# Recurrence with filler matmuls set one behind each group, and key and query work moved ahead of routing

## The reference

```
q, k, v = silu(causal_conv4(x @ Wq)), ... Wk, ... Wv;  beta = sigmoid(x @ Wb)      # x is layer-normed
q, k = l2norm per head;  per chunk: M = I + tril(beta k k^T, -1);  u, w = M^-1 (beta v), M^-1 (beta k)
per chunk in sequence:  u -= w S;  o = q S + tril(q k^T) u;  S += k^T u
y = rmsnorm(o) @ Wo;  x2 = x + layernorm(y);  h = layernorm(x2)
router: sigmoid scores, 3 of 8 groups, 4 of 32 experts, weights;  shared = (silu(h Wg) * (h Wu)) Wd
experts: gather by slot, silu(G) * U, down, weighted scatter-add;  out = x2 + layernorm(experts + shared)
```

## Time and profile before

| what | value |
| --- | --- |
| median of 3 executions | 1083.34 us |
| profiled execution | 1090.8 us |
| its span on the core | 1089.0 us |
| TensorE busy | 853.8 us (78%) |
| VectorE busy | 666.0 us (61%) |
| ScalarE busy | 367.1 us (34%) |
| mean granted TensorE clock | 0.892 of full |
| step part / expert part | to about 820 us / the rest |

### The profile page before, as it was taken

How to read it: one execution, slowest core, us unless ns; L and a number is a source line. 1 busy time by engine, 2 the same in 40 slices (tenths; PEclk the granted TensorE clock), 3 DMA queues, 4 the chain that set the end, 5 groups by cost and what they waited for, 6 DMA issues and landing times. The chain is left out here.

```text
span 1089.0 us, 31228 instructions
## 1 busy us (share of the span) xinstructions
PE 853.8 (78%) x13520; PEld 646.2 (59%) x13520; DVE 666.0 (61%) x1267; ACT 367.1 (34%) x683; POOL 117.5 (11%) x182
## 2 busy tenths in 40 slices
PE   6586697897889889889897988278693799999910
PEld 5465576665657676666665757146372688888800
DVE  2697498778569777977977976864238122212226
ACT  2523324533432543353453344112311112221215
POOL 1000000000000000000000000000001344454344
PEclk9886697999899989999999999779985899999965
DMA  8110002005100200200200020020006599999768
GB/s 272 62 42 2 4 1 81 4 1 201 61 5 1 100 4 2 79 23 3 69 33 2 1 81 4 1 78 4 26 33 251 190 362 361 360 346 360 253 153 241
DMA packets 48625, 113.15 MB, mean 104 GB/s; under 512 B 8576, under 2 KB 8704, under 8 KB 48368
## 3 DMA queue, kind: packets, MB, share of 16 engines
q1 hardware_dynamic: 42224, 96.50, 24.4%
q0 software_dynamic: 6272, 14.68, 6.2%
HBM read 84.34 MB, written 26.84 MB: 102 GB/s over the span
## 5 line engine op out<-in xcount | busy, mean ns | idle before, releaser
L463 PE MATMUL bank<-xnT,wring 128*128 128x256 f32 x768 | 168.9, 382 | 0.0
L463 PEld LDWEIGHTS bank<-xnT,wring 128*128 128x128 f32 x768 | 146.1, 191 | 23.7 <-issue 3.4
L1584 PEld LDWEIGHTS ps_g<-xgT,wring 128*128 128x128 f32 x1024 | 121.1, 194 | 17.2 <-issue 17.2
L1584 PE MATMUL ps_g<-xgT,wring 128*128 128x128 f32 x1024 | 121.5, 278 | 1.3 <-ACT xgT L1614 0.7
L992 DVE SCALAR_TENSOR_TENSOR cv<-pre,taps,cv 128x1024 f32<-128x1024 f32 x72 | 92.3, 1282 | 21.5 <-ACTq L757 20.3
L1717 DVE TENSOR_TENSOR hid<-ps_g,sg 128x160 f32<-128x160 f32 x32 | 10.4, 325 | 148.1 <-ACT sg L1624 104.1
L1493 POOL MEMSET xgT<- 128x512 f32 x2 | 1.0, 532 | 810.4 <-POOLq L1795 810.4
L555 PE MATMUL bank<-wo,o_ch 128*128 128x512 f32 x128 | 65.1, 667 | 20.6 <-DVE o_ch L1140 20.6
L596 PE MATMUL bank<-hT,su_w 128*128 128x256 f32 x256 | 72.8, 426 | 1.5 <-issue 1.5
L596 PE MATMUL bank<-hT,sg_w 128*128 128x256 f32 x256 | 68.3, 399 | 0.7 <-issue 0.4
L1614 ACT ACTIVATE xgT<-ps_x 128x320 f32<-128x320 f32 x32 | 14.0, 437 | 161.2 <-PE ps_x L1573 161.2
(11 more groups left out here) (189 smaller groups left out, 1420.6 us busy)
## 6 DMA issues: line engine op xcount, KB each, us to landing
wring<-in_ffn_W_gate SPq DMA_DIRECT2D x32, 512.0 KB
wring<-in_ffn_W_up SPq DMA_DIRECT2D x32, 512.0 KB
wring<-in_ffn_W_down SPq DMA_DIRECT2D x32, 512.0 KB
x_in<-in_attn_x SPq DMA_DIRECT2D x8, 512.0 KB, 3.8
x_res<-in_attn_x SPq DMA_DIRECT2D x8, 512.0 KB, 4.4
x_rows<-x SPq DMA_DIRECT2D x8, 512.0 KB, 2.8
h_rows<-h SPq DMA_DIRECT2D x8, 512.0 KB, 3.8
side_rows<-acc_sb SPq DMA_DIRECT2D x8, 512.0 KB, 5.2
```

The lines of the kernel that those rows point to most:

```text
L463: m = te.matmul(bank[:, c * COLS:(c + 1) * COLS], wqkv[:, w, kt, ct * P:(ct + 1) * P], xnT[:, kt, :], start=(kt == 0), stop=(kt == KT - 1))
L1584: m = te.matmul(ps_g[q % 2][:, (2 * a + i) * P:(2 * a + i + 1) * P], w[:, k, i * P:(i + 1) * P], xgT[q % 2][:, k, :], start=(k == 0), stop ...
```

## The change

It permutes the instruction lists of three engines and the order in which PSUM banks are handed out. No instruction is added or removed; only the places differ. `silu_kq`, `residual` and the like keep their code.

```diff
-ORDER = dict(begin="XPGX", one="PXOGW", two="PHEXFIOGW", loop="PHVYEXFIOGW", seven="PHVYEFIOGW", end="HVYEFIOWVYHEFIVY")
+ORDER = dict(begin="XPGX", one="PXOGW", two="PHEXFOGIW", loop="PHVYEXFOGIW", seven="PHVYEFOGIW", end="HVYEFIOWVYHEFIVY")
...
-        FILL = ["VVRVV", "YY", "", "YY", "EE", "EE", "", "D", "DD", "DF", "", "F", "F", "F", "", ""]
+        FILL = ["VVVVR", "Y", "Y", "Y", "Y", "E", "E", "E", "E", "D", "D", "D", "D", "F", "F", ""]
+        FILL_END = ["VVVVR", "Y", "", "Y", "YY", "E", "", "E", "EE", "D", "", "D", "DD", "F", "", "FFF"]
...
-            up(0)
-            up(1)
-            gram(s, phase, (0,))
-            up(2)
-            gram(s, phase, (1,))
-            up(3)
+            if phase != "one":
+                for q in (2, 3):
+                    shared_up(s - 2, phase, "F", 0, q)
+            gram(s, phase, (0, 1))
             output_squares(s - 1, phase)
             gram(s, phase, (2, 3))
+            if phase != "one":
+                for q in range(4):
+                    shared_up(s - 2, phase, "F", 1, q)
             out_proj(s - 1, phase)
```

ScalarE's body:

```diff
                 take_h(s - 2, phase)
-                take_scores(s - 2)
             if phase in ("loop", "seven"):
                 take_shared(s - 3, phase, 0)
+            if phase != "one":
+                take_scores(s - 2)
             take_new(s - 1, 0)
+            take_output(s - 1, 0)
+            silu_factor(s, 1)
+            if phase != "seven":
+                rstd(0, s + 1)
+            take_new(s - 1, 1)
             if phase in ("loop", "seven"):
                 take_shared(s - 3, phase, 1)
-            take_output(s - 1, 0)
-            silu_factor(s, 1)
-            take_new(s - 1, 1)
             take_output(s - 1, 1)
+            silu_factor(s, 0)
+            take_new(s - 1, 2)
             if phase != "one":
                 gate_factor(s - 2, phase, 0)
-            silu_factor(s, 0)
-            take_new(s - 1, 2)
             take_output(s - 1, 2)
             silu_factor(s, 2)
-            if phase != "seven":
-                rstd(0, s + 1)
```

VectorE's body (`first_norm` is split into `first_moments` and `first_scale`; `masks` takes its columns; `hidden` of half 0 is split):

```diff
             next_state(s - 1, 0)
-            conv_begin(0, s)
+            if phase != "seven":
+                first_moments(s + 1)
             residual(s - 1, 1)
-            conv_end(0, s)
-            if phase != "one":
-                route_scores(s - 2)
+            conv(1, 0, s)
+            if phase != "seven":
+                first_scale(s + 1)
             next_state(s - 1, 1)
             conv_begin(2, s)
             residual(s - 1, 2)
             conv_end(2, s)
             if phase != "one":
-                route_groups(s - 2)
+                route_scores(s - 2)
             next_state(s - 1, 2)
             if phase != "one":
-                hidden(s - 2, phase, 0)
+                hidden_gate(s - 2, phase, 0)
+                route_groups(s - 2)
             residual(s - 1, 3)
-            if phase != "seven":
-                first_norm(s + 1)
             silu_v(s)
+            turn_v()
+            if phase != "one":
+                hidden_up(s - 2, phase, 0)
             next_state(s - 1, 3)
             silu_kq(0, 1, s)
             silu_kq(1, 0, s)
             output_sums(s - 1)
+            turn_k()
+            masks(s, phase, (0, 1))
             if phase != "one":
                 hidden_gate(s - 2, phase, 1)
+            masks(s, phase, (2, 3))
+            scale_output(s - 1)
+            problems()
+            if phase != "one":
                 route_experts(s - 2)
+            row_weights(s)
+            if phase != "one":
                 hidden_up(s - 2, phase, 1)
-            scale_output(s - 1)
-            turn_k()
-            turn_v()
-            masks(s, phase)
-            problems()
-            row_weights(s)
-            inverse_diagonal(range(1, 8))
+            inverse_diagonal(range(1, 12))
             rows_moments(s - 1, phase)
-            inverse_diagonal(range(8, 12))
-            mean_shift(1, s - 1)
             inverse_diagonal(range(12, HB - 1))
             column_weights()
+            mean_shift(1, s - 1)
             turn_first()
+            below_times_first(0)
             rows_residual(s - 1)
-            below_times_first(0)
             below_times_first(1)
```

More of the change, by code:

```diff
@@ L625, in fill @@
                     return
-                for c in FILL[n]:
+                for c in (FILL_END if phase == "end" else FILL)[n]:
                     if c == "R":
@@ L649, in body @@
                 turn_x(s + 1, phase)
-            def up(q):
-                if phase != "one":
-                    shared_up(s - 2, phase, "F", 1, q)
-            up(0)
-            up(1)
-            gram(s, phase, (0,))
-            up(2)
-            gram(s, phase, (1,))
-            up(3)
+            if phase != "one":
+                for q in (2, 3):
+                    shared_up(s - 2, phase, "F", 0, q)
+            gram(s, phase, (0, 1))
             output_squares(s - 1, phase)
             gram(s, phase, (2, 3))
+            if phase != "one":
+                for q in range(4):
+                    shared_up(s - 2, phase, "F", 1, q)
             out_proj(s - 1, phase)
@@ L920, in _ @@
         take_h(STEPS - 2, "end")
+        take_shared(STEPS - 3, "end", 0)
         take_scores(STEPS - 2)
-        take_shared(STEPS - 3, "end", 0)
         take_new(STEPS - 1, 0)
-        take_shared(STEPS - 3, "end", 1)
         take_output(STEPS - 1, 0)
         take_new(STEPS - 1, 1)
+        take_shared(STEPS - 3, "end", 1)
         take_output(STEPS - 1, 1)
+        take_new(STEPS - 1, 2)
         gate_factor(STEPS - 2, "end", 0)
-        take_new(STEPS - 1, 2)
         take_output(STEPS - 1, 2)
@@ L976, in moments, with first_moments, first_scale @@
             last.then_inc(stats_ready[n], 1)
-        def first_norm(s):
+        def first_moments(s):
             dve.wait_ge(x_loaded, 16 * (s + 1))
             moments(0, s, [x_in[:, b, :] for b in range(B)])
+        def first_scale(s):
             dve.wait_ge(rs_ready[0], s + 1)
@@ L984, in first_norm @@
             last.then_inc(xn_ready, 1)
+        def first_norm(s):
+            first_moments(s)
+            first_scale(s)
         def conv(a, w, s):
@@ L1023, in turn_k, with masks @@
             link(v.transpose(k_tok[:, :, :], kq[:, :, 0, :]))
-        def masks(s, phase):
+        def masks(s, phase, columns=range(J)):
             first, st = where(phase, "G", s)
-            for j in range(J):
+            for j in columns:
                 ring.wait_full(dve, first, st, j)
```

## The result

The changed kernel takes 1067.15 us, the median of 4 executions (1061.95 to 1069.99), against 1083.13 for the kernel before in the same comparison; the ratio is 0.9848, 95% interval 0.9805 to 0.9890. Forecast were 1052 and a range of 1029 to 1066: the direction was right, the gain half of what was forecast, and the median lies 1 us outside the range. Between the two profiled executions, against which the sum was made, the gain is 20.8 us (1090.8 to 1069.99), not 31.5.

The account below looks back on a forecast made before the run. VectorE's fixed 34 us plus first residual to `row_weights`, paced by instruction supply, bound a body. Gains 5.9 + 4.6 + 2.6 + 13.8 + 4.6 = 31.5 us took the median from 1083.3 to about 1052; own range 1043 to 1061, with (a) and (b) 1029 to 1066.

Parts of the forecast that it names:

- What bounds the kernel: Steady body: some 34 us of VectorE work plus the time from first residual to `row_weights`, which the change can shorten.
- From turn_x to `row_weights`: Steady body, counted from the handover to `row_weights`: 22.9 us before, 19.2 after, a gain of 3.7.
- the handover: Instruction supply's delivery at the last output group's issue gap, 31.7 us after the first solve; forecast 0.9 earlier.
- The supply's place: Recurrence: instructions come 512 at a time, every 8 us or so; supply at 30.8 us sets when Gram products start.
- rival (a): Recurrence: supply is no limit with even fillers, engines alone set it; 7.9 us a body, 1030 in all; chance 0.12.
- 26.9 of content that I had counted for TensorE: Recurrence: TensorE's work from first solve to last output group's end, without idle and with two F letters moved out.
- Rival (b): Recurrence's end: supply no earlier or half-clock stretch longer; 2.6 us a body, 1064 in all; chance 0.22.
- Some 34 us, which the change only permutes: VectorE from L1041 to the next body's first residual: norms, inverse and `scale_v`, length unchanged.
- Body 3: First solve waits for take_scores, now behind the zero-fill's wait: about 2.0 us lost, 2.6 net gain.
- The drain: The program's "end" part: the supply gap again sets its last group, so gain 0.
- (c): Recurrence: sigmoids on ScalarE's queue delay take_new; 24 us slower, 1107 in all; chance 0.06.
- (d): Whole body: the out_proj to h to first solve chain sets it, nothing is won, 1083; chance 0.03.

Follow-up runs that it names:

- e11: Kernel before with only the changed kernel's ScalarE and VectorE lists, but take_scores ahead of take_shared(0); TensorE's list and bank order old: 1069.52 us, ratio 0.9861.
- e8: Changed kernel with 128 unread records ahead, take_scores ahead of take_shared, and the drain's gating of half 0 behind residual(3): 1044.70 us, ratio 0.9581.

## Why the prediction was half right

**What bounds the kernel: right in the main.** The way from the first residual through `row_weights` held the gain, and the lists of VectorE and ScalarE alone give 15 us by the ratio, 18 by the medians (e11). Within it VectorE still waits for TensorE: 1.85, 1.08 and 2.33 us ahead of the three later residuals of body 5.

**From turn_x to `row_weights`: right in size, in part by luck.** I had 3.7 us from the handover; measured in body 5, from the start of turn_x: 22.7 before (488.33, behind the last output matmuls of the earlier trace rows, to 511.03), 18.9 after (471.07 to 490.01), so 3.8. Like for like my figure was 19.05: 19.2 with the 0.6 of turn_x and without hidden_up's 0.75, which the new list has behind `row_weights`. But it had no gap in it, and the measured 18.9 has two in the Gram groups, 1.74 and 0.23. With 128 records ahead, where these gaps are gone, the stretch takes 16.7 to 17.0. Body 1 gave 6.9 against 5.9, body 2 4.3 against 4.6.

**The supply's place: wrong, and the error of mechanism.** The step was "Supply, at 30.8, is the longest of the three and sets when the Gram products start; TensorE and VectorE wait inside". That a gap recurs with the record count was right, and rival (a), no limit, fell. But I took it for a clock of 512 records and asked only when the last handover comes. The borders stand every 256 records, and what a gap costs depends on the group in which it falls. With the new filler list three fell into the update groups, in the path of the cycles. By my count turn_x should have started 30.2 us after the first solve (30.8 less the 0.6 of turn_x ahead of the handover). It started 31.8, 32.8 and 31.6 us after it in bodies 4 to 6, and 30.5, 30.3 and 30.9 with 128 records ahead, where the update groups are free of gaps. In the mean of bodies 4 to 6 this is 1.4 us of gain that is missing, as much as the whole body lacks. In body 5 (438.27 to 471.07), 5.9 us lie above the 26.9 of content that I had counted for TensorE: 4.0 of gaps in three update groups and, the rest, mostly the half clock behind the third.

Rival (b) had about the size (2.6 a body, 1064 in all) and a wrong reason: supply was not late at the end, it was in the way in the middle. The Trainium skill ("Runtime: NRT & Kernel Launch", Instruction fetch mechanics) says that instructions come in blocks of 256 and that crossing a border is mostly hidden. The runs agree with the 256, by the places of the gaps, and the trace has 98 transfers for 40 gaps. But what is not hidden counts: the issue idle of TensorE's rows between 80 and 790 us adds up to 44.2 us in the changed kernel and 20.0 with 128 records ahead, and between these two profiled executions the time falls by 23 us (1069.99 to 1046.73).

**"Some 34 us, which the change only permutes": not quite.** hidden_up of half 1 stood ahead of `row_weights` (498.17) and now stands behind it. My sum had its 0.75 in the stretch ahead; it costs 1.0 here, so 0.25 a body is missing.

**Body 3: right.** take_scores behind the zero-fill was put at 2.0; the first cycle took 19.8 us instead of 17.9.

**The drain: wrong, and about as large.** "The supply gap again sets its last group, 0" missed that VectorE waits for a filler ahead of residual(3). The drain cost 5.3 us, half of the 10.7 by which the 20.8 us fall short of the 31.5; bodies 4 to 7 fall short by 6.0. Some 3.3 us are this wait; the gap and the slow key/state group ahead of it are in it as well. e8 wins 2.4 us back up to that residual, with 128 records ahead. I had read FILL_END only for its letters' number, not for who waits for slot 12.

**From the profile to the median.** I subtracted the whole sum from the median. The profiled execution of before was 7.7 above its median, that of after 2.8 above: 4.8 us of the 20.8 is not in the medians. The kernel before also ranged from 1078 to 1094 in later executions. I did not see this in three.

**(c) and (d)** did not happen: take_new starts within 0.2 us of each solve's end in body 5, and the longer 34 us stretch has 0.24 us of idle behind hidden_up and no other new gap.

## What to carry to other kernels

Before a long run of small matmuls is rearranged, list the profile's issue gaps by the group and the matmul in which they fall: a permutation that costs nothing by engine times can move them from a harmless group into the path. Compare two such versions at several numbers of records ahead; one number measures luck as well, here up to 21 us of 1067. And where a queue gets a wait for a filler, look up in which slot that filler stands, in every phase of the program.

## What the runs showed that I had not expected

128 records that nothing reads, put where TensorE is idle anyway, took 21 us off the changed kernel and some 15 off the kernel before; 256 records left the gaps in their places and took 5 off.

The gaps end 1.2 to 1.6 us after a transfer of 16384 bytes on the instruction queue in the kernels before and after, and 1.2 to 1.7 us after one in all the others. What makes a gap long is mostly a transfer that starts late. For the 2.62 us ahead of 488.12 in the kernel before, it started 0.23 us before TensorE ran dry and took 1.39 us; for the 0.23 us ahead of 481.68 in the changed kernel, it started 2.06 us before and took 0.93. What sets the start of a transfer, and with it why the gaps are also shorter in sum at a good place (20.0 us against 44.2), is open: the waits of TensorE for the state, behind the output group, may give the supply time, but no run separates that. Nor does any show why 256 records give 1062 and none 1067, with gaps in nearly the same places but 31.7 us in sum. The profiled execution there is the fastest of its kernel, and that of the changed kernel its slowest; the changed kernel's own executions spread by 8 us.
